# Decay exponents of a state-space layer capped after the exponential instead of before it, with a new instruction order

## What is computed

```
dt = softplus(dt_in + dt_bias);  A_bar = exp(-exp(A_log) * dt)
h  = A_bar * h + (dt * B_t) x_t ;   y_t = C_t . h
y  = rmsnorm(y + Dp * x) * silu(z);  out = y @ out_proj_w
```

## Time and profile before

| what | value |
|---|---|
| median of three runs | 4044.49 us |
| profiled execution, its own time | 4028.71 us |
| its span, first to last instruction | 4027.1 us |
| mean granted TensorE clock | 0.973 |
| PE busy | 3741.4 us (93%) |
| DVE busy | 3082.5 us (77%) |
| ACT busy | 2793.7 us (69%) |
| POOL busy | 2523.8 us (63%) |
| DMA, mean | 76 GB/s |

### The profile page before, as it was taken

The page is one execution under the profiler, slowest core; times in us unless marked ns, Lnnn a source line. Parts: engine busy times, 40 slices in busy tenths (PEclk is TensorE's granted clock), DMA queues, the critical chain, the costliest instruction groups (busy, mean ns, idle before and its releaser), DMA issues.

```text
span 4027.1 us, 119475 instructions
## 1 busy us (share of the span) xinstructions
PE 3741.4 (93%) x34582; PEld 2920.7 (73%) x34583; DVE 3082.5 (77%) x8792; ACT 2793.7 (69%) x8434; POOL 2523.8 (63%) x3252
## 2 busy tenths in 40 slices
PE   5999999999999999979978999999999999999997
PEld 4888888888888888867755666666666666666664
DVE  5888888888888888845546777777777777777775
ACT  4778777778888788844436666767667666766764
POOL 4566655656666566622236777777777777777774
PEclk8999999999999999979989999999999999999998
DMA  4334432333333333324420111111011111111110
GB/s 132 134 116 125 137 123 95 115 116 100 111 117 117 116 108 108 113 74 146 144 90 26 34 32 31 34 31 34 28 33 32 32 33 31 34 30 31 32 30 17
DMA packets 222650, 304.24 MB, mean 76 GB/s; under 512 B 57216, under 2 KB 176256, under 8 KB 222592
## 3 DMA queue, kind: packets, MB, share of 16 engines
q1 hardware_dynamic: 197632, 249.83, 19.5%
q0 software_dynamic: 19200, 52.45, 4.0%
q10 hardware_dynamic: 5760, 1.24, 0.2%
HBM read 239.18 MB, written 64.23 MB: 75 GB/s over the span
## 4 chain that ended last, share of the span: by engine, by line
PE 39%; issue 21%; DVE 16%; POOL 10%; ACT 9%; DVEq 2%; DMA 1%; ACTq 1%; POOLq 0%; SPq 0%
PE Q L1553 10%; PE Q L1546 8%; PE Q L1558 5%; PE Q L1933 3%; PE Q L1779 3%; PE Q L1587 3%; POOL arena L673 2%; DVE mx L1135 2%; PE Q L1791 2%; ACT arena L1348 2%; POOL arena L681 1%; ACT arena L1345 1%; PE Q L1874 1%; POOL arena L678 1%; ACT arena L1342 1%
## 5 line engine op out<-in xcount | busy, mean ns | idle before, releaser
L1558 PE MATMUL Q<-ident,arena 128*128 128x128 f32 x3488 | 587.5, 285 | 109.8 <-ACT arena L1282 34.3
L1558 PEld LDWEIGHTS Q<-ident,arena 128*128 128x128 f32 x3488 | 408.3, 143 | 350.0 <-issue 168.3
L1553 PE MATMUL Q<-Wkvl,arena 128*128 128x512 f32 x1024 | 520.8, 601 | 1.5 <-ACT arena L1497 0.8
L673 POOL TENSOR_TENSOR arena<-arena 128x1024 f32<-128x1024 f32 x256 | 481.6, 1902 | 37.0 <-DMA arena<-cum_rows 36.7
L744 POOL TENSOR_TENSOR l<-l,half_pow 128x8 f32<-128x8 f32 x192 | 317.5, 1654 | 146.0 <-DVE l L1154 145.9
L1466 ACT ACTIVATE arena<-Q,mx 128x128 f32<-128x128 f32 x1024 | 359.8, 386 | 6.2 <-DVE mx L1135 6.2
L1381 ACT ACTIVATE arena<-Q,mx 128x128 f32<-128x128 f32 x1024 | 287.2, 386 | 101.5 <-DVE mx L960 97.3
L1546 PE MATMUL Q<-arena,Win 128*128 128x128 f32 x2560 | 347.6, 280 | 1.3 <-DVE arena L890 1.3
L1587 PE MATMUL Q<-ident,arena 128*128 128x128 f32 x2048 | 322.9, 282 | 22.2 <-ACT arena L1381 12.1
L1546 PEld LDWEIGHTS Q<-arena,Win 128*128 128x128 f32 x2560 | 324.9, 196 | 6.3 <-DVE arena L890 2.0
L914 DVE TENSOR_TENSOR arena<-arena,Q 128x1024 f32<-128x1024 f32 x256 | 311.8, 1218 | 14.0 <-ACT arena L1336 7.0
(11 more groups left out here) (292 smaller groups left out, 10195.7 us busy)
## 6 DMA issues: line engine op xcount, KB each, us to landing
arena<-cum_rows SPq DMA_DIRECT2D x256, 512.0 KB, 6.3
arena<-routed_rows SPq DMA_DIRECT2D x144, 128.0 KB, 2.0
expert_rows<-arena POOLq DMA_DIRECT2D x144, 128.0 KB, 2.0
arena<-in_x_dram SPq DMA_DIRECT2D x128, 128.0 KB, 4.4
arena<-in_ctx_dram SPq DMA_DIRECT2D x128, 128.0 KB, 3.0
x_rows<-arena SPq DMA_DIRECT2D x128, 128.0 KB, 1.7
arena<-x_rows SPq DMA_DIRECT2D x128, 128.0 KB, 2.1
out_dram<-arena SPq DMA_DIRECT2D x64, 128.0 KB, 1.7
```

Source lines behind the costliest of these rows:

```text
L673: tell(g.tensor_tensor(E8[j], E8[j], cums[:, 8 * j:8 * j + 8].unsqueeze(2).broadcast_to([P, 8, T]), ALU.subtract), "diff")
L1553: last = mm(out, lhs(c), rhs(c), start=c == 0, stop=c == n - 1)
L1558: last = nc.tensor.transpose(out[:, c * P:(c + 1) * P], src[:, c * P:(c + 1) * P], ident[:, :])
```

## The change

- The minimum of `Nc0`, the three absolutes and the semaphores `gap` and `cap` go. ACT has four steps `Ne0` to `Ne3`, each a plain exponential of `cum[t] - cum[s]`.
- `Nm0` to `Nm3` become scalar_tensor_tensor: the minimum with 1, and then the product with the masked CB.
- `cum_rows` doubles. `Dco` stores each head's row twice: once as it is (`kept`), once with both halves holding its second half (`late`). Each `Ncb` step issues two reads of 64 partitions: partitions 0 to 63 read `kept`, 64 to 127 read `late`. For s >= 64 and t < 64, which the mask zeroes, the exponent is now that of t + 64. So no exponent spans more than 64 time steps on the side where it is positive.
- All five orders of the first phase are new. In a body of SP, `Dco` is now last and `Xm Yc` stand ahead of `Ncb0`. On POOL `Nd1` stands ahead of `Mln1`. On PE `Zz Zzh` come first, and `Nv0 Nv1` stand before `Ppv0`, `Nv2 Nv3` after `Dcum`, and `Oss` before `Fr`.

```diff
@@ ORDER[1]
         "SP": """
-            Ncb0 Yc Ncb1 Mx Ncb2 Ncb3 Gm Ox Xm Dco Go
+            Xm Yc Ncb0 Mx Ncb1 Ncb2 Ncb3 Gm Ox Go Dco
         "POOL": """
-            Nd0 Mln1 Nd1 Nd2 Nd3 Wln2 Gsc Fln3 Osq Oyg Wx1r Orms
+            Nd0 Nd1 Mln1 Nd2 Wln2 Nd3 Gsc Fln3 Osq Oyg Orms Wx1r
         "DVE": """
-            Mln1 Gtop Mln1v Nc0 Wln2 Wln2v Gwt Gslot Gsn Nm0 Zgz Ghg Ddt Nm1 Dsp Ghh Dsr Yk Dss Dsz Ds7 Ds6 Ds5 Nm2 Ds4 Gxo Ds3 Pho Ds2 Phm Ds1 Ds0
-            Phx Dsd Fln3 Dsa Nm3 Fln3v Wq Vcv1 Oy Xm0 Xm1 Vcv2 Oss Fr Vcv3 Fri Bcb Frs Vxs2 Xm2 Xm3 Ox1 Vxdt
+            Wln2 Mln1 Gtop Wln2v Mln1v Gwt Gslot Gsn Nm0 Nm1 Ghg Ghh Zgz Yk Ddt Nm2 Dsp Dsr Dss Dsz Ds7 Ds6 Ds5 Gxo Ds4 Ds3 Nm3 Pho Ds2 Phm Ds1 Phx
+            Ds0 Dsd Fln3 Dsa Fln3v Wq Vcv1 Oy Vcv2 Vcv3 Oss Xm0 Xm1 Vxs2 Fr Fri Frs Ox1 Bcb Vxdt Xm2 Xm3
         "ACT": """
-            Pt0 Ne0 Mln1 YcT Pt1 Ztz Ne1 Gth Mln1n Nf1 Dab Pt2 Dae Ne2 Pt3 Nf2 Wln2 POT Yv Ne3 Wln2n Nf3 Vcv Dcum Xmr Fln3 Fln3n Xm0 Bbc Xm1 Vcth Frx
-            Xm2 Xm3
+            Ne0 YcT Ne1 Mln1 Gth Pt0 Ztz Mln1n Ne2 Pt1 Pt2 Dab Xmr Dae Pt3 Ne3 Wln2 POT Yv Wln2n Vcv Dcum Fln3 Fln3n Bbc Vcth Xm0 Xm1 Frx Xm2 Xm3
         "PE": """
-            YcT Pt0 Zz Pt1 Zzh Ggu Gguh Pt2 Mln1n Yk Ddt Pt3 Yv Vip1 Ppv Ppv0 Ppv2 Gdn POT Wln2n Vip1h Wq Dcum Nv0 Nv1 Nv2 Nv3 Xs0 Fln3n Bbc
-            Fr Oss BCB Opr Xs2 Oprh VxsT Frk
+            Zz Zzh YcT Pt0 Pt1 Ggu Gguh Yk Mln1n Yv Ddt Pt2 Gdn Pt3 Ppv Nv0 Nv1 Ppv0 Ppv2 Vip1 POT Wln2n Vip1h Wq Dcum Nv2 Nv3 Xs0 Fln3n Bbc Oss Fr
+            Opr BCB Oprh VxsT Xs2 Frk
@@ SP
-                tell(sp.dma_start(rows(cum_d, b), cumT[0:NH, :]), "cum_out", 16)
+                kept, late = (cum_d[bass.ds(b, 1), k, :, :].rearrange("a h t -> (a h) t") for k in range(2))
+                tell(sp.dma_start(kept, cumT[0:NH, :]), "cum_out", 16)
+                tell(sp.dma_start(late.rearrange("h (k t) -> h k t", k=2), cumT[0:NH, HALF:T].unsqueeze(1).broadcast_to([NH, 2, HALF])), "cum_out", 16)
-                    heads8 = cum_d[bass.ds(b, 1), 8 * j:8 * j + 8, :].rearrange("a h t -> (a h t)")
-                    tell(sp.dma_start(Ew[j], heads8.partition_broadcast(P)), f"wide{j}", 16)
+                    for k in range(2):
+                        heads8 = cum_d[bass.ds(b, 1), k, 8 * j:8 * j + 8, :].rearrange("a h t -> (a h t)")
+                        tell(sp.dma_start(Ew[j][k * HALF:(k + 1) * HALF, :], heads8.partition_broadcast(HALF)), f"wide{j}", 16)
@@ DVE
-                        tell(v.tensor_scalar(Ew[j], Ew[j], 0.0, None, ALU.min), "cap")
-                    tell(v.tensor_tensor(E8[j], E8[j], Q[4][:, 3 * T:4 * T].unsqueeze(1).broadcast_to([P, 8, T]), ALU.mult), "M")
+                    tell(v.scalar_tensor_tensor(E8[j], E8[j], 1.0, Q[4][:, 3 * T:4 * T].unsqueeze(1).broadcast_to([P, 8, T]), ALU.min, ALU.mult), "M")
@@ ACT
-                tell(s_.activation(Ew[0], Ew[0], ACT.Exp), "E")
-                tell(s_.activation(Ew[1], Ew[1], ACT.Abs), "gap")
-                tell(s_.activation(Ew[1], Ew[1], ACT.Exp, scale=-1.0), "E")
...
+                for j in range(4):
+                    yield f"e{j}"
+                    done(act, "diff", b, j + 1)
+                    tell(s_.activation(Ew[j], Ew[j], ACT.Exp), "E")
```

More of the change, by code:

```diff
@@ L29 @@
 AH, AW = 16, 16
+HALF = T // 2
 NG = AH // 4
@@ L99, in two_layers @@
     x4_d = nc.dram_tensor("x4_rows", (NB, T, D), F32)
-    cum_d = nc.dram_tensor("cum_rows", (NB, NH, T), F32)
+    cum_d = nc.dram_tensor("cum_rows", (NB, 2, NH, T), F32)
     with ExitStack() as ctx:
@@ L273, in two_layers @@
         Q = [ctx.enter_context(nc.psum_tensor(f"Q{i}", [P, 512], F32)) for i in range(8)]
-        for n in ("xa_in", "xr_in", "cum_out", "wide0", "wide1", "wide2", "wide3", "ctx0_in", "mask0_in", "meta_out", "xo_out", "meta_in", "x2s_in", "ctx1_in", "mask1_in", "x4_out", "x4t_in", "out_done"):
+        for n in ("xa_in", "xr_in", "ctx0_in", "mask0_in", "meta_out", "xo_out", "meta_in", "x2s_in", "ctx1_in", "mask1_in", "x4_out", "x4t_in", "out_done"):
             sig(n, 16)
         sig("scattered", 32)
+        for j in range(4):
+            sig(f"wide{j}", 32)
+        sig("cum_out", 32)
         sig("gathered", 32)
@@ L301, in two_layers @@
         signals("O", "POOL", "sq yg rms")
-        for n, k in (("gap", 3), ("cap", 1), ("E", 4)):
-            sig(n, k)
+        sig("E", 4)
         signals("Y", "DVE", "k0c")
@@ L489, in N @@
                     if j == 0:
-                        done(sp, "cum_out", b, 16)
+                        done(sp, "cum_out", b, 32)
                     was(sp, "Yk", b, j + 1)
-                    heads8 = cum_d[bass.ds(b, 1), 8 * j:8 * j + 8, :].rearrange("a h t -> (a h t)")
-                    tell(sp.dma_start(Ew[j], heads8.partition_broadcast(P)), f"wide{j}", 16)
+                    for k in range(2):
+                        heads8 = cum_d[bass.ds(b, 1), k, 8 * j:8 * j + 8, :].rearrange("a h t -> (a h t)")
+                        tell(sp.dma_start(Ew[j][k * HALF:(k + 1) * HALF, :], heads8.partition_broadcast(HALF)), f"wide{j}", 16)
             def O(b):
@@ L671, in N @@
                         done(pool, "cums", b)
-                    done(pool, f"wide{j}", b, 16)
+                    done(pool, f"wide{j}", b, 32)
                     tell(g.tensor_tensor(E8[j], E8[j], cums[:, 8 * j:8 * j + 8].unsqueeze(2).broadcast_to([P, 8, T]), ALU.subtract), "diff")
@@ L904, in N @@
             def N(b):
-                for j in (0,):
-                    if j == 0:
-                        yield "c0"
-                        done(dve, "diff", b, 1)
-                        tell(v.tensor_scalar(Ew[j], Ew[j], 0.0, None, ALU.min), "cap")
                 for j in range(4):
@@ L1305, in D_ @@
                 done(act, "cumps", b)
-                was(act, "cum_out", b, 16)
+                was(act, "cum_out", b, 32)
                 was(act, "diff", b, 4)
@@ L1333, in N @@
             def N(b):
-                yield "e0"
-                done(act, "cap", b, 1)
-                tell(s_.activation(Ew[0], Ew[0], ACT.Exp), "E")
-                yield "e1"
-                done(act, "diff", b, 2)
-                tell(s_.activation(Ew[1], Ew[1], ACT.Abs), "gap")
-                yield "f1"
-                done(act, "gap", b, 1)
-                tell(s_.activation(Ew[1], Ew[1], ACT.Exp, scale=-1.0), "E")
-                yield "e2"
-                done(act, "diff", b, 3)
-                tell(s_.activation(Ew[2], Ew[2], ACT.Abs), "gap")
-                yield "f2"
-                done(act, "gap", b, 2)
-                tell(s_.activation(Ew[2], Ew[2], ACT.Exp, scale=-1.0), "E")
-                yield "e3"
-                done(act, "diff", b, 4)
-                tell(s_.activation(Ew[3], Ew[3], ACT.Abs), "gap")
-                yield "f3"
-                done(act, "gap", b, 3)
-                tell(s_.activation(Ew[3], Ew[3], ACT.Exp, scale=-1.0), "E")
+                for j in range(4):
+                    yield f"e{j}"
+                    done(act, "diff", b, j + 1)
+                    tell(s_.activation(Ew[j], Ew[j], ACT.Exp), "E")
             def Y(b):
```

## The result

The changed kernel takes 4144.7 us (median of 4 runs, 4141.2 to 4151.3); the kernel before takes 4043.7 on the same chip (4 runs). The ratio is 1.0247, 95% interval [1.0232, 1.0262]: 2.5% slower, where I had forecast 1.2% faster and given the slower side 0.29. The time is also above my range. The profiled execution takes 4151.3 (span 4149.7), 122.6 more than that of before; from the first to the last cumulative sum on TensorE (63 bodies) it takes 1782.7 instead of 1676.9, so 106 of it are in the first phase.

What follows compares the result with a forecast made beforehand. TensorE sets the 26.10 us body; without three waits 24.96, plus 0.35 and 0.1 of new ones, taken as 25.3. At 0.8 less over 62 bodies, -50 us, the forecast is 3995 us, range 3945 to 4085.

Steps and rivals of the forecast that it cites:

- removed absolutes: ScalarE loses three absolutes of 1.06 us, 3.2 of its 21.4 us a body; pays only through the order.
- new multiply: VectorE's L914 as scalar_tensor_tensor, mask in PSUM: taken at 1.22 us, at most 1.38 by the nearest row.
- rival D: VectorE's changed multiply takes 2 ns an element: no body under 27 us, +56, 4100 us; chance 0.03.
- From Dcum to the next Zz: Stretch of TensorE's body: 12.18 us falls to 10.1, with a new wait of 0.3 to 0.45 for Oss.
- No wait stands in front of Pt0: On TensorE the softmax wait of 0.33 us goes, since Pt0 has Zz and Zzh ahead of it.
- Rival B: GpSimd runs Nd0 before Vxs2 if wide0 lands within 3.1 us: body 26.4, +19, 4063 us; chance 0.04.
- The halves: Wide reads split into halves of 64 partitions: 10.2 us instead of 9.5 at the upper cost, later reads 1 to 2 late.
- from Zz to Dcum: Stretch of TensorE's body: 14.9 us without waits, plus a wait of 0.1 for the softplus chain, the least certain step.
- rival A: The decay loop over wide1's landing binds: with L = 8.4 body 26.8 us, +43, 4088 us; chance 0.20.
- 18.4 + L: Loop from Dcum over wide1 to the next Dcum, in us, L being wide1's landing: 24.3 at L = 5.9.
- Rival E: Half-clock stretches cost 2.36 us each; ten more or fewer are 24 us; comes with any case, no chance given.

Runs made afterwards that it cites:

- e18: The changed kernel unedited, on chip F, against the kernel before: ratio 1.0091.
- e1: The changed kernel with each wide read as one DMA over 128 partitions, from the late copy only, on chip B; ratio to the kernel before 1.0042.
- e14: The changed kernel with whole reads of 128 partitions, from the late copy only, on chip E; ratio to the kernel before 1.0155.
- e13: The changed kernel unedited, on chip E, against the kernel before: ratio 1.0234.
- e8: The changed kernel with GpSimd's step of the first layer norm ahead of the second subtraction, on chip C; ratio to the kernel before 1.0135.
- e5: The changed arithmetic and second store in the engine orders of before, with whole reads of the late copy, on chip C; ratio to the kernel before 0.9988.
- e6: The changed kernel with whole reads and an extra half-megabyte DRAM-to-DRAM transfer per body that nobody waits for, on chip C; ratio to the kernel before 1.0043.
- e3: The changed kernel with GpSimd's scatter moved some 5 us earlier, right behind the norm's step, on chip B; ratio to the kernel before 1.0511.
- e15: The changed kernel with GpSimd's scatter moved right behind the norm's step, on chip E; ratio to the kernel before 1.0460.
- e7: The changed kernel with the input projection's first half between Nv1 and the attention products on TensorE, on chip C; ratio to the kernel before 1.0166.

## Why the prediction was wrong, step by step

**Right.** The removed absolutes and the new multiply (1.221 us; rival D fell). From Dcum to the next Zz I worked out 10.1 and a wait of 0.35; it takes 10.30 in the median at full clock on A and on F, and Oss waits 0.16 by its bracket. No wait stands in front of Pt0. Rival B didn't come: wide0 lands far too late for it.

**The halves.** I took 10.2 us instead of 9.5 for the reads and no cost a body. From the start of the first packet to the end of the last, whole reads take 8.6 (8.5 in the kernel before) and halves 10.2, and a packet of 4096 bytes takes 280 ns in the median instead of 159. That is the direction of the Trainium skill (SBUF — State Buffer, Door 1: The DMA port swizzle), which lets a transfer to 64 partitions reach half the ports, and the 10.2 us are near the 10.5 that I estimated from its figures. Yet in settled bodies wide0 lands at 9.7 behind Dcum with halves (e18) as with whole reads (e1, 9.8), wide1 at 12.5 instead of 12.2 (medians). On one chip the whole reads are 0.8% faster (e14 against e13, 32 us), most of it in the early bodies: 28.0 instead of 28.8 there, and 28.0 instead of 28.2 in the settled ones.

**The step that failed: from Zz to Dcum, 14.9 and a wait of 0.1.** In bodies wholly at full clock it takes 16.07 in the median on F and 17.75 on A, where I had 15.0. The work was summed rightly: the shortest such stretch on F is 14.93. What I had wrong is the wait, for two reasons. One is rival A's loop, which binds on F as on A and gives the 1.1 that F is over. The other is the stall, which no step of my sum had, and which adds 1.7 on A.

**The loop, 18.4 + L.** I set it at 24.3 with L = 5.9, under 25.3, and gave it a price with slow halves alone. Its path was right, and L too: in the settled bodies of e18 at full clock wide1 lands 5.87 behind its first issue. Two other terms were too small. wide1 is first issued at 6.56 and not at 5.5, since both stores, the mask and the context stand ahead of the reads, and wide0 goes out at 4.5 where I had 3.7. And from the norm to Dcum it is 12.02 and not 11.0; the reciprocal of the attention stands in that chain. Together: 6.56 + 5.87 + 0.07 + 1.90 for Nd1 put the norm at 14.4, and 12.02 more give 26.4. These bodies take 26.37 in the median, 26.1 to 26.7, and Nd1 waits 0.5 to 1.2 us for wide1 in every settled body of e18. So the loop bound without slow halves, and this part of the miss doesn't depend on the chip. The remedy of rival A, the norm ahead of Nd1, was tried in e8 and gave 1.0135, beside 1.0091 for the changed kernel on another chip. There the norm waits for VectorE instead. The old order, which has no such loop, is 0.5% faster on C with whole reads (e5 against e6), but differs in more than this. So the loop is shown by its waits and its sum, and not by an edit that removes it alone.

**The stall.** It comes into the same loop: on A the norm begins at 14.39 behind Dcum, as on F, but from there to Dcum it is 13.65. The new order had put Nv0 and Nv1 ahead of the attention products and changed GpSimd's order as well, so that these products, which began 1.06 us ahead of the scatter's issue in most bodies, now mostly begin 0.3 to 1.1 behind it. I had read the scatter only as GpSimd's time; what runs beside TensorE's products was no term of my sum. But the trace that I read could not have shown me the price: it comes from an execution without the stall (last section). In phase one the stall is 81 us (1785.6 us on E against 1704.2 on F, first to last Dcum, the same kernel); in the ratio it is 1.4% (1.0234 against 1.0091), as the kernel before is slower on E too.

**The clock.** Rival E was left out of the sum as coming with any case. In e18 phase one (first to last Dcum) has 41 stretches of half clock, 150 us together, against 14 and 96 us in the trace of before; the median granted clock of its runs is 0.9685 against 0.977 for the kernel before on F. At the earlier trace rows, 2.36 us for 6.8, those 55 us more cost about 19, half of the 34.6 us by which the medians differ there. This is an estimate; no run held the clock fixed. What makes the stretches more or fewer the runs don't tell: e1 and e6, with few waits on TensorE, have 140 and 157 us, but so have e3 and e15, with the most, 167 and 195, while e8 and e7 have 85 and 96, and e5 has 58.

**What is left.** Without the stall: old order and whole reads 0.9988 (C), new order and whole reads 1.0042 (B), new order and halves 1.0091 (F). With it: 1.0155 for the new order and whole reads and 1.0234 with halves, both on E. The kernels with whole reads leave out the first copy of the rows, so they measure and don't compute the reference. None of the kernels that compute the whole reference beats the kernel before. What stays open is why some chips stall and others don't, and what of the scatter's issue holds TensorE up.

## What to carry to other kernels

When a new order slides one engine's work in time, list what stands beside it on all other engines before and after, indirect DMAs above all; an engine's timeline alone doesn't show it. Follow a loop over every landing in it, with the issues in front of each, and write out all the work between a result and the chain that it stands in. And repeat the unedited kernel beside every set of experiments: here six edits seemed to cure the stall, and on chips that have it whole reads and the input projection between left it, so did the norm first and the quarters apart in pairs of edits, and only the early scatter took it away. The old order was never run there.
